# Top-64 attention block: score masking and key scaling on GpSimd, row sums with the exponentials, weight-centred norms, paired premix, and a new order on every engine

## The reference

```python
q = l2norm((x @ Wq) by head)
k = l2norm(concat(mem_k, (x @ Wk) by head))
v = concat(mem_v, (x @ Wv) by head)
dots = einsum('bhid,bhjd->bhij', q, k) * 10.0
dots = einsum('hg,bgij->bhij', W_pre_th, dots)        # premix over heads
dots = where(causal, -max, dots)
vk = top_k(dots, 64)[..., -1:]                        # the 64th score of each row
dots = where(dots < vk, -max, dots)
attn = softmax(dots)
attn = einsum('hg,bgij->bhij', W_post_th, attn)
out = einsum('bhij,bhjd->bhid', attn, v) * head_scale
out = (out * sigmoid(x @ Wg + bg)) @ Wo
x = layernorm(x + out)
h = silu(x @ w1 * s1) * (x @ w2 * s2)
h = gelu(h @ h1 * s3); h = gelu(h @ h2 * s4)
x = layernorm(x + (h @ w3) * s5)
```

## Time and profile before

| | us |
|---|---|
| median of 3 runs (lowest, highest) | 4881.34 (4875.89, 4881.72) |
| the profiled execution's time | 4877.63 |
| its span | 4876.0 |
| busy: DVE, PE, ACT, POOL | 4285.1, 4106.7, 2775.0, 793.6 |

### The profile page before, as it was taken

One profiled execution on the slowest core, in us unless ns is written; L12 is line 12 of the kernel. 1 busy time (PEld: TensorE's weight loads), 2 busy tenths in 40 slices (PEclk: granted clock), 3 DMA queues, 4 the chain that ended last, 5 costly groups with the idle time before them and its releaser, 6 DMA issues.

```text
span 4876.0 us, 77291 instructions
## 1 busy us (share of the span) xinstructions
PE 4106.7 (84%) x20627; PEld 2852.0 (58%) x20627; DVE 4285.1 (88%) x19801; ACT 2775.0 (57%) x7389; POOL 793.6 (16%) x3035
## 2 busy tenths in 40 slices
PE   4999999568888888888888888888888888888886
PEld 3888888435555555555555555555555555555554
DVE  6888887179999999999999999999999999999995
ACT  5777776445555555555555555555555555555552
POOL 0000000111111221112121112211111211212110
PEclk8999999769999999999999999999999999999987
DMA  2000000011111111111111111111111111111110
GB/s 90 10 12 12 12 12 7 11 23 23 23 24 23 24 23 22 22 22 22 22 22 22 22 22 22 22 22 22 22 22 23 22 22 21 22 22 22 21 21 3
DMA packets 163303, 103.66 MB, mean 21 GB/s; under 512 B 73584, under 2 KB 160688, under 8 KB 162224
## 3 DMA queue, kind: packets, MB, share of 16 engines
q1 hardware_dynamic: 162864, 98.71, 9.7%
HBM read 18.97 MB, written 8.39 MB: 6 GB/s over the span
## 4 chain that ended last, share of the span: by engine, by line
DVE 42%; PE 34%; ACT 12%; issue 5%; SPq 3%; DMA 2%; POOL 1%; DVEq 0%; ACTq 0%; POOLq 0%
DVE W L1349 17%; DVE top L1353 12%; PE bank L209 6%; PE bank L374 5%; PE bank L965 3%; ACT SN L1176 3%; DVE T L1360 3%; SPq L873 3%; PE bank L1037 2%; PE bank L342 2%; PE bank L175 2%; PE bank L987 2%; DVE top L1374 2%; DMA T<-SN 2%; PE bank L977 2%
## 5 line engine op out<-in xcount | busy, mean ns | idle before, releaser
L1353 DVE MAX8 top<-W 128x8 f32<-128x252 f32 (+11 forms) x4704 | 1387.8, 334 | 3.3
L1349 DVE MATCH_REPLACE8 W<-top,W 128x252 f32<-128x252 f32 (+13 forms) x3936 | 1278.5, 331 | 0.1
L977 PE MATMUL bank<-T,pre 128*128 128x12 f32 (+31 forms) x2048 | 542.8, 349 | 280.5 <-ACT T L1182 158.4
L977 PEld LDWEIGHTS bank<-T,pre 128*128 128x128 f32 x2048 | 357.6, 207 | 618.6 <-ACT T L1182 274.0
L1182 ACT ACTIVATE T<-bank 128x12 f32<-128x12 f32 (+31 forms) x1024 | 288.9, 282 | 515.6 <-PE bank L977 514.3
L1494 POOL TENSOR_SCALAR posts<-post,share 128x128 f32<-128x128 f32 x1024 | 365.4, 375 | 1154.5 <-DVE share L1325 1154.5
L987 PE MATMUL bank<-posts,T 128*128 128x128 f32 (+7 forms) x2048 | 461.6, 314 | 65.0 <-POOL posts L1494 61.9
L1176 ACT ACTIVATE SN<-bank,rq 128x260 f32<-128x260 f32 (+1 forms) x1024 | 365.5, 430 | 193.6 <-PE bank L965 171.5
L672 DVE TENSOR_TENSOR_SCAN hs<-dA,dx 128x256 f32<-128x256 f32 x512 | 350.4, 684 | 131.0 <-issue 99.4
L1510 POOL TENSOR_TENSOR T<-T,w_mask 128x8 f32<-128x8 f32 x1024 | 188.4, 205 | 1452.8 <-ACT T L1182 1452.8
L987 PEld LDWEIGHTS bank<-posts,T 128*128 128x128 f32 (+7 forms) x2048 | 298.9, 184 | 196.3 <-POOL posts L1494 126.4
(11 more groups left out here) (224 smaller groups left out, 8222.3 us busy)
## 6 DMA issues: line engine op xcount, KB each, us to landing
T<-SN SPq DMA_DIRECT2D x32, 130.0 KB
x_in<-in_xT SPq DMA_DIRECT2D x32, 128.0 KB, 2.3
x_mid<-x_b SPq DMA_DIRECT2D x32, 128.0 KB, 1.7
xb<-x_mid SPq DMA_DIRECT2D x32, 128.0 KB, 2.1
out_y<-x_d SPq DMA_DIRECT2D x32, 128.0 KB, 3.2
T<-SN SPq DMA_DIRECT2D x32, 126.0 KB
T<-SN SPq DMA_DIRECT2D x32, 122.0 KB
T<-SN SPq DMA_DIRECT2D x32, 118.0 KB
```

What stands on the lines that cost most here:

```text
L977: pe.matmul(MIX[:, 0:seen_by(g)], pre[:], scores(b, g), start=True, stop=True).then_inc(premixed, 1)
L1349: dve.match_replace(work, best, src, MASKED).then_inc(ranked, 1)
L1353: dve.max(best, work).then_inc(ranked, 1)
```

## The change

It touches block 1 in the main.

- The cut. The SCALAR_TENSOR_TENSOR (L1360) goes. When a group's limit is known, GpSimd makes `off` (one comparison times a large negative number) and adds it to the scores (`cut_off`, two instructions in each of 25 groups). ACT then takes the exponentials of all groups in place, with the row sums in the same instruction. So the exponentials come behind the rounds instead of beside them. `peak` is made by ACT.
- Keys. GpSimd sums the squares by six folding additions, and scales the keys. ACT copies the raw keys out of PSUM. `ktok` and `k_sq` have two buffers, and PE's second key projection waits for the raw copies.
- Norms. The output weights and the last feed-forward weights are centred beforehand, and the residual comes in by a matmul with the centring matrix in the same accumulation. Mean, subtraction, the residual additions and DVE's added epsilon go; ACT copies the centred values and adds the epsilon.
- Premix, `t_keep`: two groups at once, 16 of them instead of 32.
- Feed-forward. The scales are multiplied into the weights by GpSimd during block 0, so that ACT's and DVE's passes there are 512 wide, half as many.
- The value rows of the last four keys are made once for all sequences, stored in device memory and loaded per sequence (`V2`); PE's third value tile goes.
- `q_sum` writes four column tiles of the PE array, summed in `q_turn`.
- `posts` has 8 buffers instead of 4, `neg` 4 instead of 2; the DMA queue has one more load per sequence.
- A period has 128 beats, and tables say where each step stands on each engine.

```diff
-    SLOT, PERIODS, KM = 8, SEQS + 2, HEADS * MEM
+    SLOT, PERIODS, KM = 16, SEQS + 2, HEADS * MEM
...
+    PE_MIX = (32, 48, 64, 77, 96, 112, 130, 138)
+    PE_PREMIX = [[77, 81, 85, 89, 93, 97, 101, 105], [113, 117, 119, 121, 123, 127, 127, 127]]
+    ACT_WIDE = (21, 32, 48, 64, 80, 94, 112, 128)
+    ACT_NARROW = (20, 36, 52, 68, 84, 100, 118, 134)
+    POOL_WIDE = (14, 27, 43, 59, 67, 91, 107, 123)
+    POOL_K_SUM = (0, 2)
+    POOL_K_SCALE = (12, 20)
...
             if t:
-                pe.wait_ge(k_scaled, 4 * b + f + 1)
+                pe.wait_ge(k_raw, 4 * b + f + 1)
...
-            pe.matmul(MIX[:, 0:seen_by(g)], pre[:], scores(b, g), start=True, stop=True).then_inc(premixed, 1)
+            pe.matmul(MIX[:, 0:pair.shape[-1]], pre[:], pair, start=True, stop=True).then_inc(premixed, 1)
...
+        def exps(b, i, pair):
...
+                if g not in WHOLE:
+                    act.wait_ge(cut_made, cuts_before(b, i, j) + 1)
+                act.activation(scores(b, g), scores(b, g), ACT.Exp, bias=peak[k % 2][:, j:j + 1],
+                               accum_out=total[k % 2][:, j:j + 1]).then_inc(e_made, 1)
...
+        def k_square(b, t, f):
+            n = 4 * b + 2 * t + f
+            act.wait_ge(k_made, n + 1)
+            if t:
+                act.wait_ge(k_reduced, 2 * b + 1)
+            act.activation(sq[:, f, :], FRONT[f][:], ACT.Square).then_inc(k_squared, 1)
+            if t == 0 and b:
+                act.wait_ge(k_turned, 4 * b)
+            act.activation(ktok[t][:, f * 512:(f + 1) * 512], FRONT[f][:], ACT.Copy).then_inc(k_raw, 1)
...
-            dve.wait_ge(e_made, 4 * k + j + 1)
-            dve.wait_ge(ranked, found)
-            dve.scalar_tensor_tensor(out=s, in0=base, scalar=best[:, at:at + 1], in1=E[j][:, 0:n],
-                                     op0=ALU.is_le if turn else ALU.is_ge, op1=ALU.mult,
-                                     accum_out=total[k % 2][:, j:j + 1]).then_inc(ranked, 1)
...
+                if j == 0 and k >= 2:
+                    dve.wait_ge(cut_made, cuts_before(*divmod(k - 1, QUADS), 0))
+                    dve.wait_ge(peaked, k - 1)
...
+        def cut_off(b, i, pair):
...
+                pool.wait_ge(limited[j], len(CUTS[j]) * b + CUTS[j].index(i) + 1)
+                pool.tensor_scalar(off[j][:, 0:n], base, least, CUT, ALU.is_gt if turn else ALU.is_lt, ALU.mult).then_inc(off_made, 1)
+                pool.wait_ge(off_made, cuts_before(b, i, j) + 1)
+                pool.tensor_tensor(scores(b, g), scores(b, g), off[j][:, 0:n], ALU.add).then_inc(cut_made, 1)
...
-                if t == 15 and seq(a):
-                    dve.wait_ge(wo_made, a + 1)
-                    dve.tensor_tensor(r2[:], BACK[0][:, 0:SEQ], xb[a % NXB][:, MEM:], ALU.add).then_inc(r2_made, 1)
```

More of the change, by code:

```diff
@@ L183, in act_silu @@
         act.wait_ge(self.w1_made, 2 * k + half + 1)
-        o = self.banks["w1"][half]
-        for m in range(2):
-            mm = 2 * half + m
-            last = act.activation(self.a[:, mm, :], o[:, m * SEQ:(m + 1) * SEQ], ACT.Silu, scale=self.scale(0, mm))
-        last.then_inc(self.silu_made, 1)
+        act.activation(self.both(self.a, half), self.banks[half][:], ACT.Silu).then_inc(self.silu_made, 1)
     def pe_w2(self, pe, half, x):
@@ L220, in act_h1 @@
         act.wait_ge(self.h1_made, 2 * k + half + 1)
-        o = self.banks["h1"][half]
-        for m in range(2):
-            mm = 2 * half + m
-            last = act.activation(self.b[:, mm, :], o[:, m * SEQ:(m + 1) * SEQ], ACT.Gelu, scale=self.scale(2, mm))
-        last.then_inc(self.h1_kept, 1)
+        act.activation(self.both(self.b, half), self.banks[half][:], ACT.Gelu).then_inc(self.h1_kept, 1)
     def pe_h2(self, pe, k, m):
@@ L233, in act_h2 @@
         act.wait_ge(self.h2_made, 2 * k + half + 1)
[L234 to L238 removed]
+        act.activation(self.both(self.a, half), self.banks[half][:], ACT.Gelu).then_inc(self.h2_kept, 1)
     def pe_w3(self, pe, k):
         k += self.base
[L242 removed]
+        o = self.banks[0]
         for c in range(HC):
@@ L852, in seq, with whose @@
+    POOL_PREMIX = [[78, 82, 86, 90, 94, 98, 102, 106], [113, 117, 119, 121, 122, 123, 127, 127]]
+    def whose(p, t, beat):
+        b = p - 1 - (beat // BEATS)
+        return b if beat % BEATS == t and 0 <= b < SEQS else None
     def seq(b):
@@ L1076, in tensor @@
-                if t == 23 and seq(a):
+                for n in range(4):
+                    if t == PE_K[n] and seq(f):
+                        k_piece(f, n // 2, n % 2)
+                    if t == PE_K_TURN[n] and seq(f):
+                        k_turn(f, n // 2, n % 2)
+                    if t == PE_Q[n] and seq(f):
+                        q_piece(f, n)
+                    if t == PE_Q_SUM[n] and seq(f):
+                        q_sum(f, n)
+                    if t == PE_ATTEND[n] and seq(a):
+                        attend(a, n)
+                    if t == PE_GATES[n] and seq(r):
+                        g_piece(r, n)
@@ new lines, in tensor @@
+                if t == PE_Q_TURN and seq(f):
+                    q_turn(f)
+                for i in range(QUADS):
+                    for j in range(4):
+                        if (b := whose(p, t, PE_MIX[i] + PE_MIX_STEP * j)) is not None:
+                            mix_back(b, i, j)
+                if t == PE_OUT and seq(a):
+                    project_out(a)
+                if t == PE_VAR1 and seq(a):
+                    nc_.pe_var(pe, a)
+                if t == PE_SPREAD1 and seq(a):
+                    nc_.pe_spread(pe, a)
@@ new lines, in scalar @@
+                if t == ACT_Q_SUM and seq(f):
+                    qn_keep(f)
+                if t == ACT_Q_ROOT and seq(f):
+                    q_guess(f)
+                for i in range(QUADS):
+                    if (b := whose(p, t, ACT_PEAK[i])) is not None:
+                        peaks(b, i)
+                    if (b := whose(p, t, ACT_WIDE[i])) is not None:
+                        exps(b, i, 0)
+                    if (b := whose(p, t, ACT_NARROW[i])) is not None:
+                        exps(b, i, 1)
+                    if (b := whose(p, t, ACT_MIX[i])) is not None:
+                        at_keep(b, i)
@@ L1446, in vector @@
[L1446 to L1455 removed]
+                for i in range(QUADS):
+                    if (b := whose(p, t, DVE_SHARE[i])) is not None:
+                        share_out(QUADS * b + i)
```

773 lines of the change are left out of this document (405 added, 368 removed).

## The result

The change makes the kernel slower: 5012.48 us in the median of 4 runs (4997.06 to 5030.51) against 4880.93, a ratio of 1.0273 with a 95% interval of 1.0238 to 1.0308.

A forecast was written before the change was run, and what follows sets the result against it. DVE was taken as the bound, at 97.4 + 1.6 + 1.7 = 100.7 us per period. 986 + 116 + 30 x 100.7 + 98 + 64.5 = 4285.5, put at 4290 us for the median; range 4205 to 4450.

The forecast's parts named there:

- So the period is DVE's work and its few waits.: Kernel before, one ranking period: 119.4 us, of which DVE is busy for 112.4 and stands for 7.0.
- DVE's saving: Maskings, key sums and scaling, peaks, norm steps and gate products leave DVE: 15.0 us per period, 112.4 to 97.4.
- the waits vanish with the instructions they stand at: DVE's waits per period: 5.4 of 7.0 us go with removed instructions, 1.6 remain, 1.7 come new.
- hidden: Way from the 64th value through cut and exponential to `posts`: some 5 us of 12 per quad, while DVE does other groups.
- the ends: Outside the 30 full periods: start 986 us, first period 116, last ranking 98, end work 64.5.
- the keys' chain longer by the folds and scalings: Start, before the first ranking: this lengthening against five premix turns less, 987.6 to 986 us.
- The comparison: GpSimd's first cut instruction: about 0.96 ns a column, 340 ns at the mean 164 columns.
- The additions: GpSimd's second cut instruction, adding `off` to the scores: 2.1 ns a column, 530 ns at 164 columns.
- Rival 3: GpSimd becomes the bound and the kernel slower, from 2.6 times the new work's price; 5097 us at 2.8; chance 5%.
- Rival 1: PE becomes the bound with 94 us of work and 12 of waits: period 106, time 4449 us; chance 27%.
- The three savings: PE's work per period: premix 3.5 us less, value records 2.5 less, `q_sum` 1.9 less.
- Contention of GpSimd with DVE: GpSimd's new work slowing DVE where both run: taken as 0; at a tenth, 3.7 us per period.

The follow-up runs named there:

- b_narrow: The kernel before, with DVE's masking instruction over 8 columns instead of all and a smaller causal mask number; 4874.68 us, 0.9992.
- a_cut_dve: The changed kernel with the cut given back to DVE and exponentials again beside the rounds, so GpSimd has neither comparison nor addition; 4873.94 us, 0.9991.
- a_fold: The changed kernel with one folding addition instead of six in each key sum, so the norms are wrong; 4809.06 us, 0.9852.
- a_split: The changed kernel with a separate buffer for the first half's scores and the second half's moved ahead on PE and ACT; 4715.82 us, 0.9666.
- b_split: The kernel before, with an extra buffer for the first half's scores and the second half's moved seven beats ahead on PE and ACT; 4908.02 us, 1.0063.
- a_mult: The changed kernel with GpSimd's comparison made two products and a smaller causal mask number, so nothing is cut off; 4854.56 us, 0.9952.
- the second profile: The changed kernel, unaltered, run and profiled a second time; 5009.45 us, 1.0274.
- a_order: The changed kernel with table entries alone altered: queries' last steps and the first half's scores moved ahead; 5025.20 us, 1.0306.
- a_gates: The changed kernel with the gates' matmuls and tanh moved behind the scores, with two more ACT table loads; 5081.17 us, 1.0415.

## Why the prediction was wrong, point by point

- "So the period is DVE's work and its few waits." This step failed. It is a sum over an engine that was busy for 94% and that I took for the cause. b_narrow took 3.3 us of its work away per period and the period stayed; a_cut_dve gave it 8.2 us more and the kernel was 135 us faster. What the runs put in its place for the changed kernel is the front of a sequence, with GpSimd's queue in it: 6.7 us less there took 6.6 us off the period (a_fold), and second scores that need not wait for the first regroup DMA took off 8.6 (a_split), while DVE was busy for about 97 us per period in all three. For the kernel before the runs show only that DVE's work does not set the period. I never added up its front either; it comes to 118.7 of 119.4 us, but b_split took 7.8 us out of it and the period grew, so what sets it stays open.
- DVE's saving was right: 15.0 us predicted, 15.7 in the windows. That the waits vanish with the instructions they stand at was wrong: 7 us became 28, at other instructions. 13.0 of them are at `share`, for the way through cut and exponential that I had called hidden.
- Of the 727 us by which the span was missed, 719 lie in the 30 periods; the ends came to 1272.5 us for my 1264.5. I counted "the keys' chain longer by the folds and scalings" in the start alone. GpSimd's work on the keys is passed in each period, and a_fold shows 6.6 us per period for the folds alone. That I had no term for the chain at all is why the new order, the 8.0 us more between clip and first score, had no price either.
- The comparison was mis-sized, 0.34 us for 0.84 in the mean, because I took its price from GpSimd's product by -1. That is 12.5 us of GpSimd's time per period; taking 11 of them away again took 4.8 off the period (a_mult). The additions (0.53) and the widest fold (512 columns, 1.26 us) were right, the scaling was a little cheaper (1.04 for 1.26).
- Rival 3 had the right engine and the wrong mechanism. I asked from which price GpSimd would be full (2.6 times mine). It was 68 us of 125 busy, and its work came to 1.2 times my price. It hurt by its place in the queue.
- Rival 1, PE as the bound: PE was busy for 98 us, not 93, but a_split, with the same matmuls, ran 8.6 us per period faster. The three savings that I had counted came (premix 3.5 us, `q_sum` 2.2, values 3.6, for 3.5, 1.9 and 2.5); other matmuls took longer at a lower granted clock (0.87 for 0.92), those of the gates 487 ns (L1145) for 386 (L1037 before).
- Contention of GpSimd with DVE: none was seen. DVE's rounds took 334 and 331 ns in the mean in the second profile, as in the kernel before, with GpSimd busy for more than half the time.
- The share of the new order by itself (the 8.0 us between clip and first score and the 5.1 more in the second half's scores) was not isolated. a_order and a_gates aimed at it and missed; other orders made the kernel up to 305 us slower.

## What to carry to other kernels

Before an engine's work is taken as the period, follow one item through all engines for a whole period and add up that chain: an engine that is 94% busy can still be driven by it. Work moved to an idle engine is free only if no serial chain passes through that engine's queue; where one does, the work counts as far as it stands ahead of the chain's steps there (6.6 of 6.7 us in a_fold, 4.8 of 11 in a_mult). That such a chain fills the period does not yet show that it sets it: b_split shortened one and gained nothing. And take a little of an engine's work away in an experiment before pricing a large saving on it: where that changes nothing, something else drives it.

## What the runs showed of the hardware

On GpSimd the price of a TENSOR_SCALAR went with its pair of operations. Product and product by a per-partition limit took 428 ns in the mean over the 17 wide shapes of the cut; comparison and product 948, subtraction and product 946, on the same tiles. By shape the comparison took 741 ns at 132 columns and 1155 at 260, 3.2 ns a column, against 0.96 ns for the product by -1. The run with two products had a smaller mask number in its tiles too, but in the changed kernel, with the large one, the product by -1 took 293 ns on 128x124 and the comparison on its result 706. The Trainium skill, "GPSIMD Engine Reference", section "4.1 Engine selection", says that work with one input runs at roughly line rate there; the products agree, the comparison and the subtraction do not, and on them the measurement decides. The additions with two inputs, 530 ns in the mean, cost less than the comparison with one.

The DMA engines were busy for 0.11 of the changed kernel's periods, yet the regroup's issue took 18.4 us for the 16 transfers of the second half against 9.9 to 10.2 for the smaller ones of the first, in every kernel alike (from the first issue's start to the last one's).
